# Roots of the first edge layer on VectorE with its queues reordered, and half of the pool's dense statistics on ScalarE

## What is computed

```python
# layer 0, per edge and per node
msg = jnp.concatenate([x[row], edge_attr], axis=1)
h = jax.nn.elu(msg @ W1a + b1a) @ W1b + b1b
agg = segment_sum(h, col) / jnp.maximum(counts, 1.0)[:, None]
y = jax.nn.elu(jnp.concatenate([x, agg], axis=1) @ W2a + b2a) @ W2b + b2b
x = layernorm(x + y)
# layer 1 begins with a product with W of the new x
# layer 3, twice: sort_conv, then batch norm over all nodes
dense = the first 4 messages x[src] of each node, missing ones filled with W @ blank + b
out = einsum(sort(dense, axis=1), cw) + cb
h = a * x + out
h = (h - h.mean(0)) / jnp.sqrt(h.var(0) + 1e-5) * g + be
```

## Time and profile before

| | |
|---|---|
| median of 3 runs | 4410.17 us (4407.81 to 4410.22) |
| profiled execution, its own time | 4406.22 us |
| its span | 4404.2 us |
| busy PE, DVE, POOL, ACT | 3497.0, 3360.6, 3043.6, 2304.7 us |
| first edge layer | first `less1` at 942.7, last instruction of its norms ends at 1433.0 us |
| pool 1 | block ahead starts at 3519.8, first gather at 3524.4, last sort ends at 3772.3 us |

### The profile page before, as it was taken

One profiled execution on the slowest core, in us unless ns is written; L12 is line 12 of the kernel. 1 busy time (PEld: TensorE's weight loads), 2 busy tenths in 40 slices (PEclk: granted clock), 3 DMA queues, 4 the chain that ended last, 5 costly groups with the idle time before them and its releaser, 6 DMA issues. The chain is left out here.

```text
span 4404.2 us, 59487 instructions
## 1 busy us (share of the span) xinstructions
PE 3497.0 (79%) x14981; PEld 2181.8 (50%) x14981; DVE 3360.6 (76%) x10477; ACT 2304.7 (52%) x4672; POOL 3043.6 (69%) x2666
## 2 busy tenths in 40 slices
PE   5688888747776566499979999999699678687984
PEld 3466666624444566444435555555344367564331
DVE  6888888846666788655647888888688689787985
ACT  2498888713344577523337777777233222132752
POOL 1378888757775788677737888888577567463547
PEclk9999999979999788799989999999899889898997
DMA  3254445433332677444433443443344278694873
GB/s 86 92 146 140 138 142 148 124 98 91 96 96 75 187 203 207 143 131 143 137 116 105 133 132 125 133 132 116 106 129 133 77 233 253 142 194 132 278 235 119
DMA packets 463646, 621.80 MB, mean 141 GB/s; under 512 B 71541, under 2 KB 220204, under 8 KB 463308
## 3 DMA queue, kind: packets, MB, share of 16 engines
q1 hardware_dynamic: 402700, 534.09, 38.6%
q0 software_dynamic: 54912, 83.37, 9.0%
q10 hardware_dynamic: 5696, 0.55, 0.1%
HBM read 402.95 MB, written 218.46 MB: 141 GB/s over the span
## 5 line engine op out<-in xcount | busy, mean ns | idle before, releaser
L1195 PE MATMUL ps<-big,Whh 128*128 128x512 f32 x1176 | 537.4, 593 | 0.5 <-ACT big L1400 0.5
L1615 PE MATMUL ps<-big,We 128*128 128x512 f32 x800 | 355.5, 598 | 8.4 <-DVE big L1765 4.5
L1195 PEld LDWEIGHTS ps<-big,Whh 128*128 128x128 f32 x1176 | 212.9, 191 | 214.2 <-issue 211.4
L1228 POOL TENSOR_TENSOR big<-big 128x512 f32<-128x512 f32 x196 | 248.0, 1285 | 71.5 <-ACT big L1222 71.5
L604 POOL DMA_INDIRECT me<-node_tab,ix x208 | 239.7, 1152 | 70.8 <-issue 48.3
L611 POOL DMA_INDIRECT meta<-me,rank_ix x208 | 223.4, 1074 | 63.1 <-issue 60.5
L1765 DVE SCALAR_TENSOR_TENSOR big<-r2N,zN 128x512 f32<-128x512 f32 x400 | 254.0, 686 | 9.9 <-ACT zN L1676 6.2
L1213 DVE SCALAR_TENSOR_TENSOR big<-ps,bhh,hid 128x512 f32<-128x512 f32 x196 | 146.4, 747 | 141.2 <-ACT hid L1206 137.4
L1615 PEld LDWEIGHTS ps<-big,We 128*128 128x128 f32 x800 | 150.8, 191 | 195.1 <-issue 188.7
L688 PE MATMUL ps<-big,hotrow 128*128 128x256 f32 x832 | 201.5, 398 | 22.5 <-ACT hotrow L746 12.1
L1238 POOL TENSOR_TENSOR big<-big 128x512 f32<-128x512 f32 x98 | 141.5, 1464 | 109.1 <-DVE big L1233 109.1
(11 more groups left out here) (421 smaller groups left out, 11045.9 us busy)
## 6 DMA issues: line engine op xcount, KB each, us to landing
xN<-x_tab SPq DMA_DIRECT2D x196, 256.0 KB, 3.3
h_tab<-yN SPq DMA_DIRECT2D x124, 256.0 KB, 2.4
krow<-key_row SPq DMA_DIRECT2D x100, 256.5 KB, 4.4
agg<-in_xt SPq DMA_DIRECT2D x98, 256.0 KB, 3.3
big<-x_tab SPq DMA_DIRECT2D x98, 256.0 KB, 3.1
x_tab<-hid SPq DMA_DIRECT2D x98, 256.0 KB, 3.5
agg<-x_tab SPq DMA_DIRECT2D x98, 256.0 KB, 2.8
x_tab<-zN SPq DMA_DIRECT2D x98, 256.0 KB, 2.0
```

Source lines behind the costliest of these rows:

```text
L1195: last = nc.tensor.matmul(bank[:, :], Whh[:, l, c * D:(c + 1) * D], h, start=True, stop=not both)
L1228: nc.gpsimd.tensor_tensor(self.d[u], h[u], self.n[u], SUB).then_inc(self.dd, 1)
L1615: last = nc.tensor.matmul(MS[:, :], We[:, l * NTYPE + t, :], masked[g % 2][:, t, :], start=(t == 0), stop=(t == NTYPE - 1))
```

## The change

In the first edge layer `powers` leaves POOL. On DVE it is 11 linked instructions on the same 128x8 numbers: an initial guess from the bits of the number and three Newton steps. DVE's list is put in another order, with the roots behind `residual2` and both shifts behind `stats2`. On ACT `copy_src` and `copy_dst` come first in a step, then `exp1`, and `normalise1` after it. On PE `output2` runs a step later, directly behind `turn_src`.

In pool 1 the odd dense groups go to ACT: two passes over the turned group, Identity and Square with the mean of the first group taken off, each with a sum as accumulator output. DVE keeps the even ones, one after its first instruction and one in the middle. The small block ahead is gone: its work on DVE (`prepare`), PE and POOL is at the head of pool 1, where POOL sets the ones behind its first gathers. `coefficients(0)` joins both halves of the statistics.

```diff
-                        after(pool, x1_d, min(s - 2, EGR - 1))
-                        after(pool, x2_d, s - 4)
-                        nc.gpsimd.tensor_tensor(rsq[s % 2][:, :], veq[s % 2][:, :], mhalf[:, 0:2 * J], ALU.pow).then_inc(rstd_d, 1)
-
                     gather_src(0)
-                    for k in range(EGR + 5):
-                        staged(k - 3, EGR + 2, powers)
+                    for k in range(EGR):
                         staged(k + 1, EGR, gather_src)
...
 
@@ -2014,14 +2006,14 @@
                             last = nc.tensor.matmul(O2[:, spans[j]], x1T[g % 2][:, spans[j]], WL1[:, :], start=True, stop=True)
                         last.then_inc(out2_d, 1)
 
-                    for k in range(EGR + 3):
...
                         staged(k - 2, EGR, output1)
                         staged(k, EGR, hidden1)
                         staged(k - 1, EGR, turn_dst)
                         staged(k - 1, EGR, hidden2)
                         staged(k - 3, EGR, turn_x1)
-                        staged(k - 3, EGR, output2)
 
                 @block.scalar
                 def _(act):
@@ -2075,10 +2067,10 @@
                         last.then_inc(x2_d, 1)
...
+                        staged(k, EGR, exp1)
                         staged(k - 3, EGR, normalise1)
-                        staged(k, EGR, copy_src)
-                        staged(k, EGR, exp1)
-                        staged(k - 1, EGR, copy_dst)
                         staged(k - 5, EGR, normalise2)
                         staged(k - 1, EGR, exp2)
                         staged(k - 3, EGR, copy_x1)
...
                     nc.vector.memset(agg[1][:, :, :], 0.0).then_inc(scan_d, 1)
                     for q in range(2):
                         nc.vector.memset(veq[q][:, :], 1.0).then_inc(set_d, 1)
+                    links = [0]
+
+                    def link(ins):
+                        links[0] += 1
+                        ins.then_inc(root_d, 1)
+                        dve.wait_ge(root_d, links[0])
+
+                    def powers(s):
+                        dve.wait_ge(set_d, 2)
+                        after(dve, eps1_d, min(s, EGR - 1))
+                        after(dve, eps2_d, min(s - 2, EGR - 1))
+                        v, y, t, seed = veq[s % 2][:, :], rsq[s % 2][:, :], shq[0][:, :], shq[1][:, :]
+                        link(nc.vector.tensor_scalar(seed.bitcast(I32), v.bitcast(I32), 1, None, ALU.arith_shift_right))
+                        link(nc.vector.tensor_scalar(seed.bitcast(I32), seed.bitcast(I32), -1.0, 1597463007.0, MUL, ADD))
+                        after(dve, x1_d, min(s - 2, EGR - 1))
+                        after(dve, x2_d, s - 4)
+                        for n in range(3):
+                            guess = y if n else seed
+                            link(nc.vector.tensor_tensor(t, guess, guess, MUL))
+                            link(nc.vector.scalar_tensor_tensor(t, t, -0.5, v, MUL, MUL))
+                            last = nc.vector.scalar_tensor_tensor(y, t, 1.5, guess, ADD, MUL)
+                            if n < 2:
+                                link(last)
+                        last.then_inc(rstd_d, 1)
 
                     def inverse_roots():
-                        n = [0]
-
...
 
                     inverse_roots()
                     for k in range(EGR + 6):
+                        staged(k, EGR, same_key)
+                        staged(k - 1, EGR, add_bias)
+                        staged(k - 4, EGR, residual2)
+                        staged(k - 3, EGR + 2, powers)
+                        staged(k - 4, EGR, stats2)
                         staged(k - 3, EGR, shift1)
                         staged(k - 5, EGR, shift2)
-                        staged(k - 4, EGR, residual2)
-                        staged(k, EGR, same_key)
-                        staged(k - 1, EGR, add_bias)
...
-        ph = Phase()
-        linked, tot, made = ph.sems(3)
-        with nc.Block() as block:
-
-            @block.sync
-            def _(sp):
-                ph.clear_other(sp)
-
-            @block.gpsimd
-            def _(pool):
-                for k in range(3):
-                    last = nc.gpsimd.memset(cat[k][:, :, AT_ONE:AT_ONE + 1], 1.0)
-                last.then_inc(made, 1)
-                pool.wait_ge(made, 1)
...
-            @block.vector
-            def _(dve):
-                n = [0]
-
-                def link(ins):
-                    n[0] += 1
-                    ins.then_inc(linked, 1)
-                    dve.wait_ge(linked, n[0])
-
-                for l in range(2):
-                    for m in range(TOP):
-                        last = nc.vector.tensor_scalar(weightI[l][m], ident[:, :], val(l, CW + m), None, MUL)
-                link(last)
-                dve.wait_ge(tot, 1)
-                for l in range(2):
-                    link(nc.vector.tensor_tensor(cols[f"blankp{l}"], B[0][:, l:l + 1], val(l, BB), ADD))
-                    link(nc.vector.reduce_sum(cols["t0"], v3[:, l, CW:CW + 4], axis=mybir.AxisListType.X))
-                    link(nc.vector.scalar_tensor_tensor(cols[f"c{l}"], cols[f"blankp{l}"], cols["t0"], val(l, CB), MUL, ADD))
-                link(nc.vector.tensor_scalar(cols["nblank0"], cols["blankp0"], -1.0, None, MUL))
-
...
                     for g in range(EGR):
                         gather(g)
+                        if l == 0 and g == 0:
+                            for k in range(3):
+                                last = nc.gpsimd.memset(cat[k][:, :, AT_ONE:AT_ONE + 1], 1.0)
+                            last.then_inc(cat_set, 1)
 
                 @block.tensor
                 def _(pe):
+                    if l == 0:
+                        for m in range(2):
+                            last = nc.tensor.matmul(B[0][:, m:m + 1], W3[:, m, :], val(m, BLANK), start=True, stop=True)
+                        last.then_inc(blanks, 1)
...
                     def turn_dense(n):
                         after_ring(pe, bn_in, n, 16)
-                        after(pe, bn_d, n - 2)
+                        after(pe, bn_a if n % 2 else bn_d, n // 2 - 1)
                         for j in range(J):
...
+                    def dense_sums(n):
+                        after(act, bn_t, n)
+                        act.wait_ge(centred, 1)
+                        at = n // 2
+                        for c, what in ((0, ACT.Identity), (1, ACT.Square)):
+                            last = nc.scalar.activation(dense_tile(junk_bn[at % 2][c], n), dense_tile(BN[1][:, :], n), what, bias=minus_c,
+                                                        accum_out=sums[:, c, at:at + 1])
+                        last.then_inc(bn_a, 1)
+
+                    if l == 0:
+                        act.wait_ge(prepared, 8)
                     for k in range(EGR + 3):
...
                         staged(k, EGR, keep)
+                        for n in bn_of(k - 1):
+                            if n % 2:
+                                dense_sums(n)
                         staged(k - 2, EGR, rows)
 
...
-                        src = BN[n % 2][:, :]
-                        if n == NG - 1:
-                            src = src.rearrange("p (j q) -> p j q", j=J)[:, :, 0:TAILP]
-                        nc.vector.bn_stats(stat3[:, n * 6:n * 6 + 6], src).then_inc(bn_d, 1)
+                        at = n // 2 * 6
+                        nc.vector.bn_stats(stat3[:, at:at + 6], BN[0][:, :]).then_inc(bn_d, 1)
+                        if n == 0:
+                            dve.wait_ge(bn_d, 1)
+                            nc.vector.bn_aggr(first_mv, stat3[:, 0:6]).then_inc(centre, 1)
+                            dve.wait_ge(centre, 1)
+                            nc.vector.tensor_scalar(minus_c, first_mv[:, 0:1], -1.0, None, MUL).then_inc(centred, 1)
 
...
                         done = lambda n: dve.wait_ge(net, STEPS * g + n)
-                        extra = list(bn_of(g))
+                        extra = [n for n in bn_of(g) if n % 2 == 0]
...
                         nc.vector.scalar_tensor_tensor(one, at, 1.0, win[u][:, 0:WID], ALU.is_ge, MUL).then_inc(net, 1)
-                        for n in extra[0:2]:
+                        for n in extra[0:1]:
                             dense_stats(n)
...
                         nc.vector.scalar_tensor_tensor(high2, at[:, 2:WID], 2.0, high[:, 0:GR], ALU.is_ge, MUL).then_inc(net, 1)
-                        for n in extra[2:4]:
+                        for n in extra[1:2]:
                             dense_stats(n)
...
                     if l == 0:
-                        link(nc.vector.bn_aggr(f3[:, 5:7], stat3[:, :]))
+                        half, n_even = f3[:, 44:46], NG // 2 * GR
+                        share, rest = n_even / N, (N - n_even) / N
+                        link(nc.vector.bn_aggr(half, stat3[:, :]))
```

(22 more changed lines are left out.)

37 lines of the change are left out of this document (22 added, 15 removed).

## The result

| | before | after |
|---|---|---|
| median | 4409.1 us (4407.8 to 4410.2) | 4359.2 us (4357.1 to 4365.2) |
| ratio, 95% interval | | 0.9889 (0.9872 to 0.9906) |
| span of the profiled execution | 4404.2 us | 4355.3 us |
| ahead of the first `less1` | 942.7 | 942.6 (-0.1) |
| first `less1` to last | 449.8 | 414.0 (-35.8) |

The change gains 49.9 us where 26.6 were forecast. The lines of the table are starts and ends read from the two timelines; they add up to the 48.9 by which the spans differ.

A forecast was written before the change was run, and what follows sets the result against it. Edge layer bound by a loop of waits, with POOL's lateness and the clock; pool 1 by DVE. Edge layer -20, tail +7, pool 1 -9.4, block ahead -4.2: -26.6 from 4406.2, plus 4.0 for the median: 4383.6 us, range 4354 to 4408.

The forecast's parts named there:

- a POOL without pauses in the edge layer: Edge layer: listed among the signs that would show the prediction wrong; no size given.
- The loop of 17.65: Edge layer: summed waits from `less1` to `less1` give 17.65 us a step, against 18.09 and a mean of 19.17 before.
- I take the clock to fall as often as before: Edge layer: PE's clock falls in one step of three, costing 1.6 us, so 0.55 a step; 18.2 a step.
- POOL's step at 16.8: Edge layer: without `powers`, POOL's work with gather issue falls from 18.5 to 16.8 us a step.
- The roots at 0.20 a link, covered: Edge layer: 11 linked DVE instructions, 2.2 us, fit in DVE's 5.0 us idle, which falls to about 3.
- The tail, 7 lost (4 to 10): Edge layer's closing steps: roots in a row with other work lose 2 us in each of three steps and one more.
- Pool 1 at 8.7: Pool 1: 8.7 us a step instead of 9.09; 24 steps x 0.39 is 9.4 us gained (0 to 17).
- `coefficients`, nothing: `coefficients(0)`: half of a 2.81 us aggregate goes, eight links of 0.19 come; no net change.
- The loops are free: Rival: clock never falls at a pause of 2.0 and pool 1's store lands early; 12 and 7 us more, 4365; chance 0.20.
- GpSimd binds the edge layer: Rival: POOL's 12 gathers meet a busier DVE, 18.8 us a step, gain there 8 less the tail; 4396; chance 0.15.
- Nothing left: Rival: clock falls every step, store's loop stays at 9.1, only 4.2 left against a tail of 7; 4410; chance 0.10.
- The gathers starve: Rival, pool 1: gathers blocked beside DVE's two-input sort instructions, 10.5 us a step instead of 9.09; 4427; chance 0.13.

The follow-up runs named there:

- edge_order: Kernel before with only ScalarE's edge-layer list reordered (copies first, normalisation last) and `output2` a step later; roots stay on GpSimd: 4403.7 us, ratio 0.9973.
- exp_first: Changed kernel with one line of ScalarE's edge-layer list moved, `exp1` ahead of `copy_dst`: 4341.1 us, ratio 0.9844.
- gathers_aligned: Kernel before, in pool 1 a group's gathers wait for the first sort instruction of the group two earlier: 4551.6 us, ratio 1.0105, on the stalling chip.
- odd_banks: Changed kernel with pool 1's odd groups' turned tiles alternating between two PSUM banks: 4339.5 us, ratio 0.9845.
- stats_dve: Changed kernel with all four statistics of a pool 1 step again on VectorE: 4509.9 us, ratio 1.001, on the stalling chip.

## Why the prediction was right, and where it was not

**The side and, in the main, the mechanism** were right: the loop that was laid out is the one measured. The clock's part was wrong, and a sign that the prediction had named for being wrong, a POOL without pauses in the edge layer, did come. The time lies 24 us below the forecast and inside the range, but with luck: the bounds that the prediction names for the edge layer and for pool 1 end at 4364 (12 and 7.6 below 4383.6), not at the 4354 written down, and 7 us of the gain come from code that didn't change. By the spans 22.3 us more were gained than forecast: 17.5 in the loop of the edge layer (11.6 the clock, the rest the loop itself), 5.1 in pool 1 and 7 in unchanged code, less 2.1 in the first steps, 2.9 in the tail and 3.0 ahead of pool 2. Step by step:

- *The loop of 17.65.* Measured 17.38. Its terms differ by at most 0.3: `hidden1` 3.44 for 3.70, the turn until the copy 0.64 for 0.49, `elu2` 9.58 for 9.71. Over the 21 steps that is 37.9 instead of the 32 without clock losses; the first three steps gave 2.1 back.
- *"I take the clock to fall as often as before", 0.55 a step.* This is the term that failed, 11.6 us: past the first steps, from 1000 to 1350 us, the clock never fell. I had put the late roots and the clock down as two causes and kept one of them. In the trace of before the matmuls of `hidden1` are slow only behind a pause of 2.40 to 2.44, and that pause was the late roots. But the length of this pause doesn't decide alone. Of the 21 pauses ahead of `hidden1` between 1000 and 1390 us, eight are of 1.2 and none of them is followed by slow matmuls; thirteen are of 2.4, and only six of these are. The step ahead of the earlier trace rows is one of the others:

```profile
1195.56 1.13 PE L1970 MATMUL ps<-xT,W1a 128*128 128x512 f32 x2 [2.41 <-ACT big L2033]
1196.52 1.02 PE L1971 MATMUL ps<-big,W1a 128*128 128x512 f32 x2
```

  So "the 2.40 at which it fell" is not a limit that the rows show. `edge_order` shows the tie of lateness and clock from the other side: it keeps the roots on GpSimd and has the clock at 0.90. The pauses of 1.50 and 1.46 were left at full speed, so the place I took for doubtful ("about 2.0") was also sized 0.5 too long. On the chip with the stalling ACT the same code ran at 0.86 to 0.91, with pauses of 3.1 to 4.0 ahead of `turn_src` where the change has 1.50: there the term exists.
- *POOL's step at 16.8.* Measured 17.4, all of the loop's 17.38: with no `powers` left, the gathers themselves take 13.8 us and not the 13.2 that were left after it.
- *The roots at 0.20 a link, covered.* Right: 0.20 apart, DVE's idle time 2.9.
- *The tail, 7 lost (4 to 10).* 9.9, at the edge: from one chain of roots to the next 13.0, 9.5 and 9.5 us pass, in which the mechanism is as told, but `output2` also ran at 1.2 GHz twice (2.08 for 1.16).
- *Pool 1 at 8.7.* Without its first two steps the mean is 8.68. Right, though one part was off: I took 1.5 for the sums of one odd group; the passes start 0.66 apart and the read of the accumulator lasts 0.20, of which all but 0.09 is overlapped, so 1.3.
- *Starved steps.* Missed: I multiplied 24 steps of 9.09 by 0.39 and left the 6.8 us of waits in both kernels. The trace of before has four steps of 10.95 to 11.25, that of after two at the start of 10.4 and 10.8. What the 22 even steps don't give, 5 of the 14.5 us, comes from there.
- *The block ahead, 4.2.* Measured 4.4.
- *`coefficients`, nothing.* 3.0 lost: after the last sort instruction 11.3 us pass until the aggregate instead of 8.7. The weighing of the group before the last ends 7.3 us behind the start of the last sort where it ended 5.1 behind it, and what follows it is unchanged. The aggregate itself fell from 2.81 to 1.48, and the added links took it back.
- *Unchanged code.* 7 us of the gain lie in code that didn't change (pool 2, the stages between, the rest). The profiles of other kernels scatter by as much.

**The rivals.** *The loops are free* (4365) is nearest: true of the clock, not of the store, which still made `keep` wait in 12 steps. *GpSimd binds the edge layer* was wrong for the change, since PE waits for no rows there, but only just: POOL has no wait in the steady steps, and `exp_first` runs into it 0.3 us further on. *Nothing left* was also summed wrong, 4410 + 7 - 4.2 is 4413. *The gathers starve* did not come, for a reason that I had named and not weighed: DVE's pauses, or rather the turn behind them, let POOL wait and start each group at the step's head. That this place is what spares them is argued, not shown. `gathers_aligned` shows that the mechanism and its size are real. The rule of the Trainium skill (GPSIMD Engine Reference, Key points), that GpSimd contends with VectorE instructions with two SBUF inputs, agrees with the 4.50 in that trace. That section doesn't say when: in the step of the change above a gather lies wholly beside such instructions and takes 1.07.

## What to carry to other kernels

When an engine's lateness and a falling clock stand in the same rows, find out whether one causes the other before giving each a term; take the lateness away and the clock may go with it. Before moving work to another engine, write down what will stand between its inputs and its outputs in that engine's list and in the next one's: here one line of ScalarE's list decided between 1.6% faster (`exp_first`) and 2% slower. When a loop has been shortened, read at once which wait ends last now; two further moves of a line or a buffer were each worth two fifths of the change.

## What was not expected of the hardware

- A gather beside DVE's sort takes 0.94 to 1.6 us or, started at another place, 2.7 to 4.5, with nothing between in pool 1 before: 26 of 100 are long there. All 26 end 0.88 to 0.91 us, about the time of a free gather, after DVE starts its small copy of 128x3 (14 of them) or a pair of statistics from PSUM (12), the 2.72 and the 4.51 of the earlier trace rows among them, behind these two rows of before:

```profile
3655.45 1.28 DVE L2827 BATCH_NORM_STATS2 stat<-ps 128x6 f32<-128x512 f32 x2
...
3660.26 0.15 DVE L2835 COPY win<-win 128x3 f32<-128x3 f32 x1
```

  All 22 of `gathers_aligned` do the same. Yet 26 others lie wholly beside sort instructions, and 21 of these take at most 1.1. In `odd_banks`, with DVE as full, 3 of 100 are long. What decides whether a gather passes or is held until then is left open.
- An accumulated sum on ScalarE is a second instruction of 0.20 us that costs 0.09 us of time between two passes of 0.57.
- The same program took 4410 to 4412 us on two chips and 4499 on a third, with waits that the profile calls "remote", 95.6 us of them in the edge layer of `stats_dve`, 89.1 of these ACT's, and none on the others.
